# The last feed-forward of a two-layer decoder: router logits, expert masks and the final norm rearranged

## The reference, cut to what matters

```
x = layernorm(x + L1_ffn(x))                  # x: 8 x 128 x 256
gate_base, up_base = x @ Wg.T, x @ Wu.T       # 704 wide
base_out = silu(gate_base) * up_base @ Wd.T
probs = softmax(x @ Wr.T)                     # 8 experts, router logits
topw, topi = top_k(probs, 2)
for each expert e, of rank 16:                # only the two chosen count, by weight
    h = silu(gate_base + 2 x @ Ag[e].T @ Bg[e].T) * (up_base + 2 x @ Au[e].T @ Bu[e].T)
    acc += we[e] * 2 * h @ Ad[e].T @ Bd[e].T
L1_ffn = base_out + acc
```

## Time and profile before

| | us |
|---|---|
| median of three runs | 894.86 |
| the profiled execution, its time | 896.01 |
| its span, first to last instruction | 894.2 |
| PE busy in the span | 829.8 (93%) |
| DVE busy | 580.4 (65%) |
| ACT busy | 362.9 (41%) |
| POOL busy | 261.1 (29%) |
| mean granted TensorE clock | 0.964 |

### The profile page before, as it was taken

How to read it: one execution, slowest core, us unless ns; L and a number is a source line. 1 busy time by engine, 2 the same in 40 slices (tenths; PEclk the granted TensorE clock), 3 DMA queues, 4 the chain that set the end, 5 groups by cost and what they waited for, 6 DMA issues and landing times. The chain is left out here.

```text
span 894.2 us, 12889 instructions
## 1 busy us (share of the span) xinstructions
PE 829.8 (93%) x4202; PEld 615.7 (69%) x4202; DVE 580.4 (65%) x1090; ACT 362.9 (41%) x839; POOL 261.1 (29%) x234
## 2 busy tenths in 40 slices
PE   7999999999889689999999979999997896999996
PEld 5788888888544468888888868544445344778885
DVE  5667667567789675444444475788884699764534
ACT  3564555545520423333333341377774002443422
POOL 2222121223079523232323135211302983241100
PEclk9999999999979699999999999999999897899998
DMA  9301011011101301111111010000000012000001
GB/s 306 79 25 47 23 47 47 23 47 42 36 27 32 100 24 55 36 54 36 53 39 51 17 37 1 0 1 1 1 1 1 30 40 66 0 15 16 1 1 47
DMA packets 22990, 33.71 MB, mean 38 GB/s; under 512 B 2624, under 2 KB 15552, under 8 KB 22592
## 3 DMA queue, kind: packets, MB, share of 16 engines
q1 hardware_dynamic: 22944, 33.11, 12.6%
HBM read 32.05 MB, written 1.05 MB: 37 GB/s over the span
## 5 line engine op out<-in xcount | busy, mean ns | idle before, releaser
L1393 PE MATMUL bank<-xTh,ringh 128*128 128x512 f32 x420 | 177.6, 423 | 5.5 <-DVE xTl L1085 3.1
L1395 PE MATMUL bank<-xTh,ringl 128*128 128x512 f32 x420 | 166.5, 396 | 0.0
L1394 PE MATMUL bank<-xTl,ringh 128*128 128x512 f32 x420 | 166.5, 396 | 0.0
L1393 PEld LDWEIGHTS bank<-xTh,ringh 128*128 128x128 f32 x420 | 80.4, 191 | 20.6 <-issue 4.2
L1395 PEld LDWEIGHTS bank<-xTh,ringl 128*128 128x128 f32 x420 | 79.4, 189 | 18.5
L1394 PEld LDWEIGHTS bank<-xTl,ringh 128*128 128x128 f32 x420 | 79.9, 190 | 14.0
L831 ACT ACTIVATE arena<-bank 128x512 f32<-128x512 f32 x48 | 28.7, 598 | 126.7 <-PE bank L1395 126.7
L1164 DVE TENSOR_TENSOR arena<-bank,arena 128x512 f32<-128x512 f32 x48 | 33.2, 692 | 64.7 <-PE bank L1603 64.7
L1431 PE MATMUL bank<-outh,HTh 128*128 128x256 f32 x192 | 54.8, 285 | 2.3 <-DVE HTl L1169 1.3
L550 POOL CAST ringh<-ring 128x512 fp32r<-128x512 f32 x24 | 14.7, 613 | 143.0 <-PE bank L1395 143.0
L527 POOL CAST ringh<-ring 128x768 fp32r<-128x768 f32 x15 | 12.4, 827 | 150.2 <-DMA ring<-w_attn 150.1
(11 more groups left out here) (244 smaller groups left out, 1973.0 us busy)
## 6 DMA issues: line engine op xcount, KB each, us to landing
ring<-w_moe SPq DMA_DIRECT2D x24, 256.0 KB, 2.8
ring<-w_attn SPq DMA_DIRECT2D x15, 384.0 KB, 3.2
toep<-toep SPq DMA_DIRECT2D x32, 128.0 KB, 2.1
outring<-w_down SPq DMA_DIRECT2D x24, 128.0 KB, 2.0
outring<-wo_attn SPq DMA_DIRECT2D x16, 128.0 KB, 2.0
ring<-w_ffn SPq DMA_DIRECT2D x6, 256.0 KB, 3.2
wq<-w_attn SPq DMA_DIRECT2D x1, 1344.0 KB, 12.9
arena<-sel SPq DMA_DIRECT2D x1, 1152.0 KB, 7.6
```

What stands on the lines that cost most here:

```text
L1393: pe.matmul(o, ringh[:, slot, wc], xTh[:, k, halves[j]], start=(k == 0), stop=False)
L1394: pe.matmul(o, ringh[:, slot, wc], xTl[:, k, halves[j]], start=False, stop=False)
L1395: ins = pe.matmul(o, ringl[:, slot, wc], xTh[:, k, halves[j]], start=False, stop=(k == DK - 1))
```

## The change

Three things are changed. (1) The router logits of both halves are made at once, ahead of the rank products, with `Wr` (padded to 32 columns by its neighbours) as the stationary operand and four batches side by side in four column groups of the array. The result lies experts by tokens, is copied out by ACT and turned back by two PE transposes behind `rank_inputs(0)`. (2) The masks are compared at 64 numbers per partition (`pick`) and spread to 1024 by a copy; the orders of PE, ACT and DVE around them are rearranged; two of the eight low-part products move from POOL to DVE (`am_last`); POOL begins `blh` later, when all of `xTl` is done. (3) Batches 0 to 3 are finished in the units (0, 1), (2), (3): base, adapter, norm and store of a unit before the next; batch 3 gets its own bank, 4. Batches 4 to 7 no longer wait for the other sums to be scaled.

```diff
+LAST_UNITS = ((0, 2, 0), (2, 3, 1), (3, 4, 4))
 # SP
-            for j, done in ((1, ln_x0), (0, ln_x1)):
-                sp.wait_ge(done, 6 * B // 2)
-                half = slice(j * B // 2, (j + 1) * B // 2)
-                sp.dma_start(out[:, half, :], xN[:, half, :]).then_inc(out_done, 16)
+            sp.wait_ge(ln_x0, 24)
+            sp.dma_start(out[:, B // 2:B, :], xN[:, B // 2:B, :]).then_inc(out_done, 16)
+            for first, end, _ in LAST_UNITS:
+                sp.wait_ge(ln_x1, 20 + end)
+                sp.dma_start(out[:, first:end, :], xN[:, first:end, :]).then_inc(out_done, 16)
 # POOL
-            pool.wait_ge(xt_act, 17)
+            pool.wait_ge(xt_hl, 12)
             pool.tensor_copy(blh[:], lowB).then_inc(b_hi, 1)
...
-                for c in range(2):
+                for c in range(2 - m):
 # ACT
-            high_input(0)
-            high_input(1)
+            act.wait_ge(l1_psum, 1)
+            act.activation(HS[:, 3, 0:2 * S], bank[:, 4, 2 * S:4 * S], ACT.Copy).then_inc(l1_evac, 1)
             act.wait_ge(l1_sub, 1)
             act.activation(we1[:], we1[:], ACT.Exp).then_inc(l1_exp, 1)
-            high_input(2)
-            high_input(3)
-            silu1(0)
-            silu1(1)
+            for n in range(4):
+                high_input(n)
             for m in range(TOP1):
                 act.wait_ge(mask_psum, 2 * m + 2)
                 act.activation(maskT[:, m, :], bank[:, 6 + m, :].bitcast(BF16), ACT.Copy).then_inc(mask_evac, 1)
+            silu1(0)
+            silu1(1)
...
-            norm_and_turn(5, turn=False, lead=1)
+            def last_deviations(n, first, end):
+                act.wait_ge(ln_var, 11 + n)
+                act.activation(sd[:, first:end], mv[:, first:end, 1], ACT.Sqrt, bias=eps[:, 0:1]).then_inc(ln_sd, 1)
...
 # DVE
-            low_input(0)
-            low_input(1)
             dve.wait_ge(l1_done, 1)
...
-            low_input(2)
-            low_input(3)
...
-                ins = dve.tensor_tensor(maskrep[:, q, :, :, :], iotar, at, ALU.is_equal)
+                ins = dve.tensor_tensor(pick[:, q, :, :], iota1, expert_is(q), ALU.is_equal)
...
+            dve.tensor_copy(maskrep[:, 0, :, :, :], pick[:, 0, :, :].unsqueeze(3).broadcast_to([P, B, NE1, RANK]))\
                 .then_inc(mrep_done, 1)
+            link(dve.tensor_tensor(pick[:, 1, :, :], pick[:, 1, :, :], pick[:, 0, :, :], ALU.subtract))
+            dve.tensor_copy(maskrep[:, 1, :, :, :], pick[:, 1, :, :].unsqueeze(3).broadcast_to([P, B, NE1, RANK]))\
+                .then_inc(mrep_done, 1)
+            for n in range(4):
+                low_input(n)
...
-            hidden(0)
-            hidden(1)
             for m in range(TOP1):
                 for c in range(2):
                     masked_high(m, c)
+            hidden(0)
+            hidden(1)
+            for w in range(2):
+                dve.tensor_tensor(am[:, w, 1, 1, HALF:TOK], ahl[:, w, 1, HALF:TOK].bitcast(F32),
+                                  bank[:, 5, :].bitcast(BF16)[:, HALF:TOK], ALU.mult).then_inc(am_last, 1)
...
-            norm(5, bd_done, [3, 4, 1, 2], first_bank=0, lead=1)
...
+            for n, (first, end, at) in enumerate(LAST_UNITS):
+                dve.wait_ge(bd_done, 3 + n)
+                for b in range(first, end):
+                    ins = dve.tensor_tensor(last_sum[b], bank[:, at, (b - first) * D:(b - first + 1) * D], xN[:, b, :], ALU.add)
+                link(ins)
+                last_statistics(first, end, lambda b: last_sum[b])
+                dve.wait_ge(ln_sd, 12 + n)
+                link(dve.reciprocal(rstd[:, first:end], sd[:, first:end]))
+                for b in range(first, end):
+                    dve.scalar_tensor_tensor(xN[:, b, :], last_sum[b], mv[:, b, 0:1], rstd[:, b:b + 1].broadcast_to([P, D]),
+                                             ALU.subtract, ALU.mult).then_inc(ln_x1, 1)
 # PE
             def logits1(j):
                 pe.wait_ge(xt_act, 18 + 2 * j)
-                for b in range(4 * j, 4 * j + 4):
-                    for k in range(DK):
-                        ins = pe.matmul(bank[:, 4, b * NE1:(b + 1) * NE1], xT[:, k, b * S:(b + 1) * S],
-                                        wres[:, k, R_WR:R_WR + NE1], start=(k == 0), stop=(k == DK - 1))
+                for k in range(DK):
+                    for g in range(4):
+                        ins = pe.matmul(bank[32 * g:32 * (g + 1), 4, (2 + j) * S:(3 + j) * S], wres[:, k, R_WR:R_WR + NE0],
+                                        xT[:, k, (4 * j + g) * S:(4 * j + g + 1) * S], start=(j == 0 and k == 0),
+                                        stop=(k == DK - 1), skip_group_check=True)
...
-            ins = logits1(0)
+            logits1(0)
+            logits1(1).then_inc(l1_psum, 1)
             rank_inputs(0)
-            rank_inputs(1)
-            logits1(1).then_inc(l1_done, 1)
-            rank_inputs(2)
-            rank_inputs(3)
-            for k in range(2):
-                gate1(k)
-                up1(k)
+            turn_logits1()
+            for n in range(1, 4):
+                rank_inputs(n)
+            gate1(0)
             for m in range(TOP1):
                 turn_masks(m)
+            up1(0)
+            gate1(1)
+            up1(1)
...
-            for b in range(4):
-                down_base(b)
-            for b in range(4):
-                down_adapter(b)
+            for first, end, _ in LAST_UNITS:
+                for b in range(first, end):
+                    down_base(b)
+                for b in range(first, end):
+                    down_adapter(b)
```

More of the change, by code:

```diff
@@ L377, in decoder_layers @@
         wo_done = sem("wo_done")
+        l1_psum = sem("l1_psum")
+        l1_evac = sem("l1_evac")
         l1_done = sem("l1_done")
@@ L393, in decoder_layers @@
         am_lo = sem("am_lo")
+        am_last = sem("am_last")
         h_hi = sem("h_hi")
@@ L934, in _ @@
                 act.activation(WT[:, q, c * HALF:(c + 1) * HALF], bank[:, q, :], ACT.Copy).then_inc(wt_evac, 1)
-            norm_and_turn(5, turn=False, lead=1)
+            def last_deviations(n, first, end):
+                act.wait_ge(ln_var, 11 + n)
+                act.activation(sd[:, first:end], mv[:, first:end, 1], ACT.Sqrt, bias=eps[:, 0:1]).then_inc(ln_sd, 1)
+            last_deviations(0, B // 2, B)
+            act.wait_ge(ln_scale, 6)
+            for b in range(B // 2, B):
+                act.activation(xN[:, b, :], rN[:, b, :], ACT.Identity, bias=shift[:, b - B // 2:b - B // 2 + 1],
+                               scale=rstd[:, b:b + 1]).then_inc(ln_x0, 1)
+            for n, (first, end, _) in enumerate(LAST_UNITS):
+                last_deviations(n + 1, first, end)
         @block.vector
@@ L1381, in _, with last_statistics @@
                 dve.tensor_tensor(HS[:, 2 * c, :], HS[:, 2 * c, :], HS[:, 2 * c + 1, :], ALU.add).then_inc(dw_done, 1)
-            norm(5, bd_done, [3, 4, 1, 2], first_bank=0, lead=1)
+            last_sum = {b: HS[:, 1 + 2 * (b // 2), (b % 2) * D:(b % 2 + 1) * D] for b in range(4)}
+            def last_statistics(first, end, summed):
+                for b in range(first, end):
+                    ins = dve.bn_stats(st[:, b, :], summed(b))
+                link(ins)
+                for b in range(first, end):
+                    ins = dve.bn_aggr(mv[:, b, :], st[:, b, :])
+                ins.then_inc(ln_var, 1)
+            dve.wait_ge(ln_x0, 20)
+            for q in (2, 3):
+                dve.wait_ge(bd_done, q - 1)
+                ins = dve.tensor_tensor(rN[:, 2 * q:2 * q + 2, :], bank[:, q, :].rearrange("p (b d) -> p b d", b=2),
+                                        xN[:, 2 * q:2 * q + 2, :], ALU.add)
+            link(ins)
+            last_statistics(B // 2, B, lambda b: rN[:, b, :])
+            dve.wait_ge(ln_sd, 11)
+            link(dve.reciprocal(rstd[:, B // 2:B], sd[:, B // 2:B]))
+            dve.scalar_tensor_tensor(shift[:], mv[:, B // 2:B, 0], -1.0, rstd[:, B // 2:B], ALU.mult, ALU.mult)\
+                .then_inc(ln_scale, 1)
+            for n, (first, end, at) in enumerate(LAST_UNITS):
+                dve.wait_ge(bd_done, 3 + n)
+                for b in range(first, end):
+                    ins = dve.tensor_tensor(last_sum[b], bank[:, at, (b - first) * D:(b - first + 1) * D], xN[:, b, :], ALU.add)
+                link(ins)
+                last_statistics(first, end, lambda b: last_sum[b])
[4 more added lines that the diff above has]
+                                             ALU.subtract, ALU.mult).then_inc(ln_x1, 1)
         @block.tensor
@@ L1763, in logits1, with turn_logits1 @@
                 pe.wait_ge(xt_act, 18 + 2 * j)
-                for b in range(4 * j, 4 * j + 4):
-                    for k in range(DK):
-                        ins = pe.matmul(bank[:, 4, b * NE1:(b + 1) * NE1], xT[:, k, b * S:(b + 1) * S],
```

(23 more changed lines are left out.)

11 lines of the change are left out of this document (3 added, 8 removed).

## The result

Four runs of the changed kernel gave 883.15 to 886.84 us, median **884.84**; four of the kernel before gave 894.21 to 895.65, median 894.77. The ratio is **0.988** (95% interval 0.985 to 0.991), so 9.9 us less (7.9 to 13.3). The profiled execution took 883.47 us, its span 881.6 (before: 896.01 and 894.2). One execution of the kernel before that is on record with the first experiments, of 2067.69 us, is left out of the ratios; the median of 896.22 given there includes it and would be 896.10 without it.

What follows compares the result with a forecast made beforehand. PE, busy 93% of the span, was taken as the bound. Masks and entry 7.6 plus end 3.3 made 10.9 us off 896.01, giving 885.1; set to the median 884.0, plus 0.4 for the clock: 884.4 us, range 882.2 to 888.2.

Steps and rivals of the forecast that it cites:

- POOL behind xTl: Entry: blh and bll start after xTl, so xN takes 1.67 us, 1.2 less, and all depending on it comes 1.2 earlier.
- Logits: Entry: two sets in four column groups, 1.3 us each; logits with DVE at 761.3 instead of 766.8.
- rival 3: Router logits: column groups do not run side by side, 32 records take 6.8 us, masks 4.1 later; 888.5 us, chance 0.05.
- the sum above: Entry: POOL's blh and bll (1.73 + 3.49 us) run from about 757.9 to 763.2, costing nothing on POOL.
- The clock: PE's rank products: full clock back at 763, between 761.5 and 765, where it had been 765.1.
- Low parts: Masks: the first masked product starts at 773.9 instead of 778.08, 4.2 us earlier.
- Block 0: Its 24 masked products run almost closed, 5.6 us, to 779.5; DVE is what is late next.
- Rival 1: Block 0: DVE takes over, hidden(0) slips 1 to 2 us, masks gain 5.5, time 886.5 us; chance 0.2.
- The loop behind block 0: From 788.3 to 859 PE has no gap, so time gained on entry passes undiminished unless a new wait arises.
- The end: Behind the last products: smaller units and a 128 KB store end at 890.85, 3.3 us earlier (2.4 to 4.0).
- the late clock that I had put at 0.4: Profile to median: the profiled clock looks late, so part of the gain is not one against the median; 0.4 us added.
- Rival 4: Entry through masked products: small PE holes keep the clock at 1.2 GHz, making it slower; to 790 gives 897; chance 0.02.

Runs made afterwards that it cites:

- POOL early: The changed kernel with POOL's blh and bll started by the first copies of xT again, as before; 885.00 us, ratio 0.988 to the kernel before.
- the repetition: The changed kernel run again with nothing altered, beside its variants on one chip; 884.56 us against 895.81 for the kernel before, ratio 0.988.
- the halves timed apart: Two kernels: the kernel before with only the new end, 892.99 us (3.2 less); the changed kernel with the old end, 886.61 us (9.6 less).
- the front alone: The changed kernel with the old norm and two 512 KB stores at its end; 886.61 us, ratio 0.988 to the kernel before.

## Why the prediction was right, point by point

It said 884.4 us; the two medians are 884.84 and 884.56. The mechanisms stood, but for two steps named below: POOL's bll beside the moved chain, and the moment at which the clock comes back. The sum of the traces did not quite stand: 12.7 where the prediction had 10.9.

**POOL behind xTl: as forecast.** xN 1.67 us, 1.2 less, and the kernel with POOL early brought 2.88 and 5.74 back. The changed kernel's zero is 1.1 us later than that of before, so its POOL start at 759.16 and bll's end at 764.2 are 758.1 and 763.1 in the prediction's time: it had said 757.9 and 763.2.

**Logits: right form, size between the bounds or below them.** 1.3 us a set was a choice between 0.97 and 1.94. It took 1.08 at 1.2 GHz and 0.65 at 2.4 GHz; I had assumed the half clock for all of it, so my lower bound missed the second. In the repetition the logits are with DVE at 761.87, in the prediction's time 761.2; it had said 761.3. In the first trace, with the clock back early, it is 759.3. The column groups do run side by side, which ends rival 3: one by one, 32 records would have taken 6.8 us.

**"By that rule the copies would wait for bll if it were still running; it ends at 763.2 by the sum above, 1.5 us before them, so the sum stays": this step held with the late clock and failed with the early one.** The rule is the Trainium skill's, "GPSIMD Engine Reference", section "Key points": POOL and VectorE share their SBUF interfaces, with contention when VectorE's instruction uses two ports or reads two inputs from SBUF. I asked only what it would do to the two new copies, at one moment of the clock. But the cast of the indices stands 0.6 us ahead of them (in the repetition) and has the form of the row that I had quoted from the earlier trace rows; and with the early clock the chain came 2 us earlier, under a bll that did not. The trace agrees with the rule: 1.19 us beside bll, 0.20 without, 1.1 us at PE. The range of clock moments that I had for PE should have been applied to this meeting too.

**The clock: "Before, it rose 5.4 us after the 512-column products had begun (759.7 to 765.1); now these begin at 758.0. I take 763, between 761.5 and 765": this step failed for the early executions.** In the prediction's time the clock came back at 761.6 in the repetition, 3.8 us after these products began, and at 754.9 in the first trace, ahead of the logits. Of eleven traces with the new front five have it back by 4.6 us after the zero, one at 7.7, four at 11.3 and one at 13.3. "If the clock rises before 761" had a chance of 0.04, and the first trace is that case.

**Low parts: forecast 4.2 us earlier, measured 6.1 (5.2 with the late clock).** The sum had a slip: 767.7 and 2.18 make 769.9 for the masks, not 769.7, and so 4.0 us. Against the repetition the missing 1.0 is made of the ranks, which ended 0.45 earlier (the clock came back at 761.6, not at 763), the wait for DVE's low parts of the rank products (a_lo), 0.4 shorter, and the turns of the masks, 1.97 instead of 2.18 us. With the early clock 1.0 more came, net of what the cast gave back.

**Block 0: right.** 24 products were to take 5.6 us almost closed; from the low parts to down they took 5.9, in both traces, one wait of 0.55 us for hidden(0) included. Before it was 9.5. I named DVE as what is late next, and it is. Rival 1 would have made that gap 1 to 2 us; it did not. But the low parts' maker was less decisive than I thought: with all eight on POOL the time stays.

**The loop behind block 0: right.** What is gained at down (8.8 to 9.8) is gained at the end of PE: it passes on undiminished.

**The end: forecast 3.3 us, measured 3.9, within the bounds of 2.4 and 4.0.** The mechanism was right, the sizes a little high. Behind PE's end I had 2.5 to the last normalisation and 2.4 for the store; it was 2.2 and 2.3. The 128 KB store lands in 1.9 us, like the 128 KB loads of the earlier trace rows. DVE was to be free just as unit (3) arrives; it was idle for 0.71.

**Why the number came out all the same.** The traces give 1.8 us more than the sum (2.8 with the early clock) and the medians do not show it: 9.9 in the first comparison, 11.25 in the second, with intervals up to 13.3 and 13.6, and 12.8 from the halves timed apart. Part of it is the late clock that I had put at 0.4: a late clock costs the changed kernel 0.95 us (repetition against first), and an early one in some executions of the kernel before would lower its median against its profile. That last step is argued, not shown: both traces with the old front have the clock back at 14.6 to 14.7. The record speaks for it without naming the stage: of 40 executions of that kernel beside the experiments, eight have a mean granted clock of 0.968 or 0.969, and these took 889.65 to 893.30 us, against 0.964 and 896.01 of the profiled one. The correction of 1.15 us from profile to median I had made in the same spirit, and the rest is inside the scatter. So the hit to 0.4 us is partly luck: a front and an end under-estimated by 1.2 and 0.6 us (with the late clock), and medians that fell short of the traces.

**Rival 4**, a clock that stays low, had nothing for it: it is back at 2.4 GHz ahead of the low parts in each of these traces.

## What to carry to other kernels

When a chain is moved earlier, draw the other engine's long instructions on the same time axis again, and go through every instruction of the moved chain, not only the new ones: here a cast of 64 numbers fell under a 3.5 us POOL subtraction and lost a tenth of the gain. When filling a wait of PE, ask first whether the filling stands ahead of the chain that releases everything else. At the end of a kernel let the last piece be small: work and store behind the last product shrink with it. And where executions scatter by more than an edit is worth, count from a common point inside the trace and compare traces whose clock came back at the same point.

## What the runs showed of the hardware

**The clock at one place differs between executions of one kernel.** In the entry the granted clock fell to 1.2 GHz some 1.1 us after the common zero in both traces of the changed kernel, 0.5 us into PE's eight short turns, which follow an idle stretch (3.1 us in the first trace), and was back at 2.4 GHz after 3.4 us in one and 10.2 in the other. This stretch at the half clock costs less than half its length: 6.8 us more of it moved PE's end by 0.95, and by 2.1 against the trace in which bll is late. PE waits for others in a part of it (0.44 us for the last copy of xT at the late clock, 0.98 at the early one).

**An attention stage 3.4 us longer, in some executions.** From the third to the fourth norm nine traces have 155.4 to 155.6 us, three have 158.8 to 158.9. The thirteenth, POOL early, has 160.7, after a stage that was 5.2 us shorter than in the others. In the three the clock is at 1.2 GHz for some 10 us near 570 and in the thirteenth for 13.7 us from 561 on, in the nine not at all there, as the second of these rows shows (the changed kernel, then the kernel with the front alone, whose code there is the same):

```profile
566.00:577.00 11.00, 9.29 (x44) 3.78 (x45) 8.97 (x14) 4.38 (x8) 2.08 (x2) 1.00 0.00 0
```

```profile
566.00:577.00 11.00, 11.00 (x32) 4.09 (x31) 8.36 (x13) 3.38 (x6) 1.24 (x2) 0.54 0.00 0
```

PE is busy throughout in the second and gets through 32 instructions instead of 44. These 3.4 us alone are a third of the change's whole effect, and why single runs of these kernels can't rank edits of 1 us.

**A copy that repeats each of 64 bf16 numbers 16 times** takes 0.69 us for 1024 results, as long as an fp32 subtraction of 512.
